# The output projection of an attention block as seven products of halves in place of eight

## The reference, cut to what matters

```python
def attn(x, Wq, Wk, Wv, Wo, q_norm_w, k_norm_w):
    H, HKV, HD = (32, 8, 128)
    q = _rmsnorm(heads(x @ Wq.T), q_norm_w)
    k = _rmsnorm(heads(x @ Wk.T), k_norm_w)
    v = heads(x @ Wv.T)
    scores = einsum('bkgqd,bksd->bkgqs', qg, k) / sqrt(HD)
    attn = softmax(scores + alibi_and_causal_mask)
    out = einsum('bkgqs,bksd->bkgqd', attn, v)
    return out @ Wo.T                      # 4096 -> 1024
x = x + attn(mix(x, condition), ...)
x = x + ffn(cond2(x, adapter), ...)        # both folded into one 1024x1024 weight
```

## Time and profile before

| what | value |
|---|---|
| time, median of 3 runs | 2484.26 us (2482.89 to 2484.3) |
| the profiled execution's own time | 2484.37 us |
| its span, first to last instruction | 2482.6 us |
| TensorE busy | 2458.3 us, 99% |
| VectorE busy | 1543.4 us, 62% |
| ScalarE busy | 967.1 us, 39% |
| GpSimd busy | 241.9 us, 10% |
| mean granted TensorE clock | 0.997 of full |

### The profile page before, as it was taken

How to read it: one execution, slowest core, us unless ns; L and a number is a source line. 1 busy time by engine, 2 the same in 40 slices (tenths; PEclk the granted TensorE clock), 3 DMA queues, 4 the chain that set the end, 5 groups by cost and what they waited for, 6 DMA issues and landing times.

```text
span 2482.6 us, 32143 instructions
## 1 busy us (share of the span) xinstructions
PE 2458.3 (99%) x12060; PEld 2050.5 (83%) x12060; DVE 1543.4 (62%) x2814; ACT 967.1 (39%) x2545; POOL 241.9 (10%) x264
## 2 busy tenths in 40 slices
PE   7999999999999999999999999999999999999998
PEld 5888888888888888888888888888888888888887
DVE  5546666666646666675745757575764666666662
ACT  3234344444424343444424434343433444443431
POOL 0100000000200010101011000000011000000011
PEclk8999999999999999999999999999999999999999
DMA  5332222222242222222233222222224222222221
GB/s 197 119 110 77 86 84 79 84 85 86 69 138 77 92 72 82 86 77 86 83 100 117 77 85 78 91 78 85 77 78 137 85 77 90 74 83 85 77 77 51
DMA packets 64093, 221.71 MB, mean 89 GB/s; under 512 B 10012, under 2 KB 10524, under 8 KB 63940
## 3 DMA queue, kind: packets, MB, share of 16 engines
q1 hardware_dynamic: 56468, 196.80, 23.9%
q0 software_dynamic: 5888, 20.97, 2.3%
q10 hardware_dynamic: 1584, 1.88, 0.2%
HBM read 207.04 MB, written 12.58 MB: 88 GB/s over the span
## 4 chain that ended last, share of the span: by engine, by line
PE 98%; DVE 0%; DMA 0%; ACT 0%; issue 0%; POOL 0%; ACTq 0%; POOLq 0%; DVEq 0%
PE main L731 84%; PE pv_bank L899 4%; PE qt_bank L864 3%; PE s_bank L880 2%; PE s_bank L881 2%; PE pt_bank L888 1%; PE pt_bank L731 1%; PE s_bank L731 1%; PE qt_bank L731 1%; PE qt_bank L816 0%; PE s_bank L816 0%; DMA mask<-in_masks 0%; DVE ring_lo L1082 0%; DMA raw<-in_wq 0%; ACT ring_hi L910 0%
## 5 line engine op out<-in xcount | busy, mean ns | idle before, releaser
L731 PE MATMUL main<-ring_hi,act_hi 128*128 128x512 f32 x1936 | 781.4, 404 | 0.0
L731 PE MATMUL main<-ring_hi,act_lo 128*128 128x512 f32 x1936 | 758.0, 392 | 0.0
L731 PE MATMUL main<-ring_lo,act_hi 128*128 128x512 f32 x1936 | 756.2, 391 | 0.0
L910 ACT ACTIVATE ring_hi<-raw 128x1024 fp32r<-128x1024 f32 x358 | 380.7, 1065 | 178.6 <-PE main L731 163.8
L1082 DVE TENSOR_TENSOR ring_lo<-raw,ring_hi 128x1024 fp32r<-128x1024 f32 x358 | 436.7, 1221 | 4.0 <-ACT ring_hi L910 4.0
L731 PEld LDWEIGHTS main<-ring_hi,act_lo 128*128 128x128 f32 x1936 | 363.9, 188 | 79.3
L731 PEld LDWEIGHTS main<-ring_hi,act_hi 128*128 128x128 f32 x1936 | 364.7, 188 | 68.8 <-issue 1.4
L731 PEld LDWEIGHTS main<-ring_lo,act_hi 128*128 128x128 f32 x1936 | 365.4, 189 | 66.8
L731 PE MATMUL main<-ring_hi,ot_hi 128*128 128x512 f32 x1024 | 417.0, 407 | 0.0
L731 PE MATMUL main<-ring_hi,ot_lo 128*128 128x512 f32 x1024 | 400.2, 391 | 0.0
L731 PE MATMUL main<-ring_lo,ot_hi 128*128 128x512 f32 x1024 | 399.2, 390 | 0.0
(11 more groups left out here) (132 smaller groups left out, 2557.9 us busy)
## 6 DMA issues: line engine op xcount, KB each, us to landing
raw<-in_wq SPq DMA_DIRECT2D x128, 512.0 KB, 3.2
raw<-in_wo SPq DMA_DIRECT2D x128, 512.0 KB, 3.2
raw<-in_wkv SPq DMA_DIRECT2D x64, 512.0 KB, 3.2
raw<-f_scratch SPq DMA_DIRECT2D x32, 512.0 KB, 3.3
acc<-in_x POOLq DMA_DIRECT2D x16, 512.0 KB, 3.5
out_tokens<-acc POOLq DMA_DIRECT2D x16, 512.0 KB, 3.5
f_scratch<-acc POOLq DMA_DIRECT2D x16, 256.0 KB, 2.3
raw<-in_w_units SPq DMA_DIRECT2D x5, 512.0 KB, 3.3
```

What stands on the lines that cost most here:

```text
L731: mm = eng.matmul(bank, a, b, start=start and n == 0 and m == 0, stop=stop and n == len(terms) - 1 and m == 2)
L910: eng.activation(dst, src, ACT.Copy).then_inc(done[stage], 1)
```

## The change

For each pair of groups and each block the projection is a product of a left matrix (512 tokens by 1024, two groups of four heads) and a right one (1024 by 1024). The changed kernel cuts both in 2x2 halves: tokens in two and two tiles, depth in the two groups, output in two halves of 512 columns. It forms seven products of halves in place of eight (`OPS`): the left factors are quarters of the left matrix or sums of them (`s1` to `s4`), the right ones quarters of Wo or sums of them (`t1` to `t4`). Each product is one step (m = 0 to 6) of 24 matmuls: two tiles, four of 128 deep, three matmuls.

- The attention's result is copied whole (`heads`, ScalarE) into `quads`. `s3` and `s2` are formed there by VectorE, `s1` and `s4` by GpSimd. Each left factor is then split as a whole, 128x1024 (`op_hi` on ScalarE, `op_lo` on VectorE), into one of three slots of `lefts`. The split of `ot` is gone.
- `t1` to `t4` are formed in the first block alone: for each pair two times four loads of 512 KB, four additions on VectorE, and four stores to `t_scratch`; the loads and stores are issued by ScalarE's queue. Later blocks load them as weights.
- The results are added up in the main banks, of which there are four now: `v1_out`, `v7_out`, `v1_in` and `u2` are copies of a bank on ScalarE, and matmuls add onto what lies there. VectorE adds four times two banks for a pair to `acc` (`c11`, `c22`, `c21`, `c12`) where there were sixteen additions for a pair; GpSimd adds the second product to both halves of two tiles (`v7_add`).
- The units of a pair are now `kv` of the next pair behind both `q` units, and then one `o` unit of seven steps: kv, q, q, kv, o, q, q, kv, o and so on. The last `o` of a block has no `kv` ahead of it. An `o` unit needs 14 chunks of weights, two a step; the ring has six slots, and a chunk is prepared as soon as its slot is free, at most one a quarter. The high and low parts lie in one tensor, `ring`.
- The split low-rank weights and the last bias share their SBUF with `quads`, so they are stored to DRAM once and loaded back in each block (`fx_store`, `fx_load0`, `fx_load1`).

The main part of the diff:

```diff
+SLOTS = 6
+MAINS = 4
...
-          x1=4.9, low=7.2,
-          w_hi=1.2, w_lo=3.8)
+          x1=1.0, low=4.0, out=0.6,
+          w_hi=0.3, w_lo=0.9)
...
+OPS = (("11", "11", "a"), ("s3", "t3", "d"), ("12", "21", "a"), ("s2", "t2", "b"),
+       ("s1", "t1", "e"), ("22", "t4", "b"), ("s4", "22", "e"))
+QUADS = {"11": 0, "21": 1, "12": 2, "22": 3}
+LEFT = {"11": 0, "s3": 1, "12": 2, "s2": 1, "s1": 0, "22": 3, "s4": 2}
+A_SLOTS = 3
+SUM_AT = {"t1": 1, "t2": 3, "t3": 0, "t4": 2}
+LEFT_AT = (dict(s3=-9, s2=-3, s1=0.5, s4=2.5, op=(-8, -6, -2, 4.4, 8.4, 12.4, 16.4)),
+           dict(s3=-4, s2=11.8, s1=12.8, s4=15, op=(-8, -2.8, 3.9, 12.6, 14.9, 16, 18)))
...
-            out += [("q", blk, g), ("o", blk, g)]
+        out.append(("kv", blk, 0))
+        for pair in range(KV_HEADS // 2):
+            out += [("q", blk, 2 * pair), ("q", blk, 2 * pair + 1)]
+            if pair + 1 < KV_HEADS // 2:
+                out.append(("kv", blk, pair + 1))
+            out.append(("o", blk, pair))
...
+    def preparations(self):
...
+        for u, c in self.chunks:
+            first = QUARTERS * self.first_step[self.units[u]]
+            if self.units[u][0] == "o":
+                free.append(first + QUARTERS * (c // 2) + 2 + c % 2 + 1)
+            else:
+                free.append(first + QUARTERS * (TILES - 1) + c + 1)
+        for n in range(len(self.chunks)):
+            if n >= SLOTS:
+                last = max(free[n - SLOTS] + AT["w_hi"], last + 1)
+            out.append(last)
+        return out
...
+        for n in range(SLOTS, len(self.chunks)):
+            self.at(self.prepared_at[n], 0, self.prepare)
+        for pair in range(KV_HEADS // 2):
+            self.right_factors(pair)
+        for u, unit in enumerate(self.units):
+            if unit[0] == "o":
+                self.left_factors(unit)
...
+    def right_factors(self, pair):
+        start = QUARTERS * (self.first_step["o", 0, pair - 1] + len(OPS) if pair > 0 else 0)
+        def loads(c):
+            for i in range(4):
+                self.add(f"t_load{i}", pair, c)
+        def stores(c):
+            for i in range(4):
+                self.add(f"t_store{i}", pair, c)
+        for c in range(2):
+            self.at(start + 11 * c, 0.5, lambda c=c: loads(c))
+            for i, stage in enumerate(("t1", "t2", "t3", "t4")):
+                self.at(start + 11 * c, 4 + 0.8 * i, lambda c=c, stage=stage: self.add(stage, pair, c))
+            self.at(start + 11 * c, 8, lambda c=c: stores(c))
...
+    def left_factors(self, unit):
+        kind, blk, pair = unit
+        first = self.first_step[unit]
+        start, when = QUARTERS * first, LEFT_AT[pair == KV_HEADS // 2 - 1]
+        for name in ("s3", "s2", "s1", "s4"):
+            self.at(start, when[name], lambda name=name: self.add(name, blk, pair))
...
+        for m in range(len(OPS)):
+            self.at(start, when["op"][m], lambda m=m: self.add("op_hi", first + m))
+            self.at(start, when["op"][m] + 0.8, lambda m=m: self.add("op_lo", first + m))
...
+    def o_step(self, k, blk, pair, m):
+        first = self.first_step["o", blk, pair]
+        lo, hi = tiles_of(blk)[0:2], tiles_of(blk)[2:4]
+        last_pair = pair == KV_HEADS // 2 - 1
+        use = OPS[m][2]
+        for tp in range(2):
+            if m == 0:
+                self.main("mm", (k, 2 * tp), ("c11", (first + 2, tp)))
+            elif use == "d":
+                self.main("mm", (k, 2 * tp), ("v7_out", (k, tp)))
+            elif m == 4:
+                self.main("mm", (k, 2 * tp), ("c12", (first + 6, tp)))
             for c in range(2):
-                self.add("mm", k, 2 * i + c)
+                self.add("mm", k, 2 * tp + c)
...
-    def transpose_x1(self, k, blk, t):
+            if m == 0:
+                self.later(AT["out"], lambda tp=tp: self.add("v1_out", k, tp))
+            elif m == 1:
+                self.later(AT["out"], lambda tp=tp: self.v7(first, k, tp))
+            elif m == 2:
+                self.later(AT["out"], lambda tp=tp: self.add("c11", k, tp))
+            elif m == 3:
+                self.later(AT["out"], lambda tp=tp: self.add("u2", first + 4, tp))
+            elif m == 4:
...
+    def v7(self, first, k, tp):
+        self.add("v7_out", k, tp)
+        self.add("v7_add", k, tp)
+        k_b = first + 3
+        self.main("v1_in", (k_b, tp), ("c21", (first + 5, tp)), self.main_of["mm", (k, 2 * tp)])
+        self.add("v1_in", k_b, tp)
...
+                elif stage == "mm" and step(key[0])[0] == "o":
+                    k, c = key
+                    kind, blk, pair, m = step(k)
...
+                            w.wait_ge("v1_out", k - 2, tp)
+                            bank = bank_of("mm", k - 2, 2 * tp)
+                        elif m == 3:
+                            w.wait_ge("v1_in", k, tp)
+                            bank = bank_of("v1_in", k, tp)
+                        elif m == 4:
+                            w.wait_ge("u2", k, tp)
+                            bank = bank_of("mm", k, 2 * tp)
+                        elif m == 5:
+                            bank = bank_of("v1_in", k - 2, tp)
+                        else:
+                            w.wait_ge("c22", k - 2, tp)
+                            bank = bank_of("mm", k - 2, 2 * tp)
+                    w.wait_ge("op_hi", k)
+                    w.wait_ge("op_lo", k)
...
+                    n = chunk_of(k, c)
+                    weights_here(n)
+                    terms = [(lefts[:, left_slot(k), 0, tp, 2 * c + j, :], lefts[:, left_slot(k), 1, tp, 2 * c + j, :],
+                              *half_chunk(ring, n % SLOTS, j)) for j in range(2)]
+                    products(bank[:, :], terms, c == 0 and m in (0, 1), c == 1, further=True).then_inc(done["mm"], 1)
...
+                elif stage == "op_hi":
+                    k, = key
+                    kind, blk, pair, m = step(k)
+                    factor = OPS[m][0]
+                    if factor[0] == "s":
+                        w.wait_ge(factor, blk, pair)
+                    else:
+                        group, half = divmod(QUADS[factor], 2)
+                        for i in (2 * half, 2 * half + 1):
+                            w.wait_ge("heads", order.first_step["q", blk, 2 * pair + group] + i)
+                    if m >= A_SLOTS:
+                        w.wait_ge("mm", k - A_SLOTS, 3)
+                    elif m == 2:
+                        w.wait_ge(*order.x_even_left[blk, pair][:1], *order.x_even_left[blk, pair][1])
+                    elif blk == 0:
+                        for i in range(4):
+                            w.wait_ge(f"t_store{i}", pair, 1)
+                    else:
+                        w.wait_ge("mm", order.left_before[k], 3)
+                    copy(lefts[:, left_slot(k), 0, :, :, :], quads[:, LEFT[factor], :, :, :], "op_hi")
...
+                elif stage == "v1_in":
+                    k, tp = key
+                    w.wait_ge("v7_out", k - 2, tp)
+                    w.wait_ge("v1_out", k - 3, tp)
+                    copy(bank_of("v1_in", k, tp)[:, :], kept[:, 0, tp, :], "v1_in")
+                elif stage == "u2":
+                    k, tp = key
+                    w.wait_ge("mm", k - 1, 2 * tp + 1)
+                    emptied, of = order.main_before["mm", (k, 2 * tp)]
+                    w.wait_ge(emptied, *of)
...
+                elif stage.startswith("t_load"):
+                    pair, c = key
+                    i = int(stage[-1])
+                    if c == 1:
+                        w.wait_ge(f"t_store{i}", pair, 0)
+                    elif pair > 0:
+                        w.wait_ge("mm", o_step(0, pair - 1, len(OPS) - 1), 3)
+                    else:
+                        w.wait_ge("weff_mm", KT, 1, 3)
+                    eng.dma_start(sums[i][:, :], d["wo"][pair, i, c]).then_inc(done[stage], 16)
+                elif stage.startswith("t_store"):
+                    pair, c = key
+                    i = int(stage[-1])
+                    name = next(t for t in SUM_AT if SUM_AT[t] == i)
+                    w.wait_ge(name, pair, c)
+                    eng.dma_start(t_scratch[pair, int(name[1]) - 1, c], sums[i][:, :]).then_inc(done[stage], 16)
...
+                    eng.tensor_tensor(quad("21"), quad("11"), quad("21"), ALU.subtract).then_inc(done[stage], 1)
...
+                        w.wait_ge("heads", order.first_step["q", blk, 2 * pair + 1] + i)
+                    eng.tensor_tensor(quad("21"), quad("22"), quad("21"), ALU.subtract).then_inc(done[stage], 1)
+                elif stage == "op_lo":
+                    k, = key
+                    low(lefts[:, left_slot(k), 1, :, :, :], quads[:, LEFT[OPS[step(k)[3]][0]], :, :, :], lefts[:, left_slot(k), 0, :, :, :],
+                        stage, k)
...
+                elif stage == "s1":
+                    blk, pair = key
+                    w.wait_ge("s2", blk, pair)
```

(20 more changed lines are left out.)

496 lines of the change are left out of this document (310 added, 186 removed).

## The result

The changed kernel took 2666.43 us (median of 4 runs, 2656.81 to 2671.6) against 2483.93 us before (2482.89 to 2484.3): 1.0731 times as long, 95% interval 1.07 to 1.0762. The profiled execution took 2667.39 us, its span is 2665.6 us. So 87.0 us of matmuls are gone, and 270 us of something else have come: 2667.4 - 2397.3. The prediction had 169 us for it.

What follows compares the result with a forecast made beforehand. TensorE, busy 99% of the span, was taken as the bound, so every new wait is paid in full. 2484.4 - 87.0 + 144 (four blocks of 36.0) + 25 = 2566 us, range 2440 to 2600.

Steps and rivals of the forecast that it cites:

- D: Rest of a block: transposes for the f units 2.0 us; u2 (0.2 a pair) and first kv to q, together 1.3.
- E: First block alone: right factors' additions and loads make TensorE wait, 25 us (10 to 40).
- the granted clock: TensorE's clock level: should it fall in the waits, all is longer than forecast; no size given.
- The saving: Projection: 384 fewer matmuls at 0.2267 us, 87.0 us off, leaving 2397.3 us if nothing waits.
- A: Borders between units, 7 a block: scale ends late, TensorE waits about 1.6 us each, 11.2 us a block.
- B: From kv to o, 3 a block: splittings and GpSimd's s1 and s4 delay gain, 4.0 us each, 12.0 a block.
- the rival at 2507: GpSimd is in nobody's way: 21 us a block, 2507 us; chance 0.22, shared with milder borders.
- C: Last pair of a block, no kv cover: border, last prob, step 3 and step 4 waits, 9.5 us a block.
- all terms at their upper ends: Whole sum with every term at its upper bound: 44 us a block and 40 for right factors, 2613 us.
- waits pile up: Rival: VectorE doesn't recover between borders, all upper ends, above 2600 us; chance 0.03.
- the cover holds: Rival: borders cost less; 2454 us with them half-hidden, 2410 if only right factors cost; below 2479, chance 0.27.
- all terms at their lower ends: Whole sum with every term at its lower bound: 11.6 us a block and 10 for right factors, 2454 us.

Runs made afterwards that it cites:

- tuned kernel without right factors: The kernel of run 7 with the right factors' loads, additions and stores left out, quarters of Wo used instead: 2404.41 us.
- Run 5: On top of run 3, weights split two quarters apart where not needed within three quarters: 2508.12 us.
- run 2: Changed kernel with GpSimd's additions s1, s4 and v7_add over an eighth of their columns: 2569.81 us.
- run 3: Changed kernel with s1, s4 and v7_add whole on VectorE in place of GpSimd, v7_add one quarter later: 2585.32 us.
- run 7: Changed kernel with additions on VectorE, weights spread, right factors apart, last pair's step 3 left factor in halves, other places tuned: 2434.33 us.
- run 8: The kernel of run 7 with s1, s4 and v7_add back on GpSimd at the same places of the order: 2472.70 us.

## Why the prediction was wrong, step by step

The direction came out, the time did not: 2666 for 2566, outside the range. Three steps failed: the price of `u2` in D, the landing of the right factors' loads in E, and the granted clock, which had no term at all.

- **The saving** is right: 384 matmuls fewer, 0.2268 apart. The additions in the banks cost TensorE nothing, as the tuned kernel without right factors shows: 2404 us, 7 above the sum.
- **A** is right but for a little: I had 1.6 us for each border, and it was 1.22 (and another 0.23 to 0.76 before the scores of the round ahead). Run 5 shows the cause to be what the sum laid out, four splittings within four quarters, and not the load of VectorE.
- **B** is right in size, 4.4 us a border for 4.0, and in its parts too: 0.68 and 3.3 to 4.2 where the sum had 0.9 and 3.6. The earlier trace rows were the right rows. But they show a part of an instruction's overlap (0.42 of 0.56 us); in the changed kernel VectorE's rows wait for GpSimd's end entirely. I priced GpSimd as a whole at 59 us (the rival at 2507), and run 2 gave 97: I had priced the hold at `gain`, in the last pair and in D, and neither at the 448 splittings, where it makes `u2` late (25 us), nor in the clock (17 us).
- **C** is right nearly to the tenth: 1.6, 5.3 and 0.5 against 1.6 to 1.95, 5.15 and 0.47. Its 5.3 was laid out with ScalarE's two splittings and 1.7 of hold. In the rows `s2` (2.30 us) and the left factor (2.64) are both held; without the hold (run 2) 3.7 of the 5.1 us stayed, so it was worth 1.4:

```profile
1328.52 2.30 DVE L1571 TENSOR_TENSOR quads<-quads 128x1024 f32<-128x1024 f32 x1 [0.32 <-ACT quads L1121]
...
1332.60 2.64 DVE L1367 TENSOR_TENSOR lefts<-quads,lefts 128x1024 fp32r<-128x1024 f32 x1
...
1335.48 5.03 PE L926 MATMUL main<-ring,lefts 128*128 128x512 f32 x11 [5.01 <-issue]
```

- **D** was 2.0 a block and measured 4.1 for the transposes of the `f` units. Runs 2, 3 and 5 leave these waits as they were, so neither the hold nor the bunched weights alone make them; they are gone in run 7, where `c21` and `c12` stand earlier among other moves, and partly back with GpSimd in run 8. What causes them stays open. The small term for `u2`, 0.2 for each pair, was the worst of the block's: 2.2 each at the three pairs that have it. I had ScalarE's two splittings ahead of `u2` ready when it came to them. With three `raw` buffers a load can only start when the splitting three chunks back is done, and that one was held by GpSimd. The step that failed here is "0.2 for each pair", and behind it that a load was nowhere in the sum of a block.
- **E** was 25 and is 52.7. In the middle of two `q` units it came as laid out: waits of 2.5 and 2.7 us where a border has 0.25 and 1.22, 4.4 us more together with 0.7 between them, for 4.5. At the starts of the `q` units the last load lands after 9 to 14 us and not 7, the value I had put just above the slower of the earlier trace rows; the wait that this gives TensorE with `mean`, a held `rstd` and `scale` behind it I had as 2.3 us, and it was 5.7 to 6.6. The first pair, where I took 5, had 8.7 and 4.7.
- **The clock** is the step that wasn't there. I closed the prediction with "should the granted clock fall in the waits, all is longer than here" and put no number on it, though a sum with waits of 4 to 5 us at 16 places of its own had to ask. It is worth 39 us in this trace.

The misses add up: 28 for E, 29 for the clock outside it, 24 for `u2`, 8 for D and 4 for B, less 7 for A, are 86 of the 101 us; the rest has no place. All but A's err on the same side, so that "all terms at their upper ends", 2613, was no upper end: the terms that were missing had none. The rival *waits pile up* had 0.03, with nothing worked out for it but the sum of the same bounds; the time lies in its range, but by the clock and by the chain from a held splitting over a late load to ScalarE, not because VectorE failed to recover between borders. Two figures of *the cover holds* don't come from the sum either: with the right factors alone it gives 2397.3 + 25 = 2422 (2407 at their lower end) and not 2410, and 2454 is all terms at their lower ends, not half-hidden borders alone.

## What to carry to other kernels

Where the bounding engine has no slack and a change gives it waits, a wait is worth its length and, if it is long enough for the clock to fall in the rows, what the next microseconds at half clock cost: price both. An elementwise operation on GpSimd with two SBUF operands isn't free help for VectorE if VectorE reads two SBUF operands beside it; count every such row of VectorE, not the one that you look at. And when a ring gets smaller and its refills come in bursts, spread them by when they are needed: on top of the move to VectorE that gave 77 us here, and turned the idea from a loss of 183 us into a gain of 50 together with the rest.
